# Four attention layers on one core: the wide layers' output projection in half chunks, and scores issued in turn with transposes

## The reference

```
wide   (layers 0, 2): q = x Wq (16 heads of 64); k, v = ctx Wk, ctx Wv; logits get a masked bias on 4 columns
                      x = softmax(q k^T / 8 + bias) v  Wo + bo + x
narrow (layers 1, 3): q = rmsnorm(x) wq (16 heads of 32); 4 heads of k, v shared by 4 heads of q each
                      x = softmax(q k^T / sqrt(32)) v  wo + x
```

## Time and profile before

| | |
|---|---|
| median of three runs | 2080.31 us (2079.71 to 2081.9) |
| the profiled execution, its span | 2080.3 us |
| TensorE busy | 2042.1 us, 98% |
| VectorE, ScalarE, GpSimd busy | 1389.7, 966.4, 644.7 us |
| main stage: wide step without, with projection | 11.35 to 11.41 us, 33.85 us |
| narrow step with one projection chunk | 10.51 us |

### The profile page before, as it was taken

How to read it: one execution, slowest core, us unless ns; L and a number is a source line. 1 busy time by engine, 2 the same in 40 slices (tenths; PEclk the granted TensorE clock), 3 DMA queues, 4 the chain that set the end, 5 groups by cost and what they waited for, 6 DMA issues and landing times.

```text
span 2080.3 us, 31294 instructions
## 1 busy us (share of the span) xinstructions
PE 2042.1 (98%) x11546; PEld 1764.4 (85%) x11546; DVE 1389.7 (67%) x2408; ACT 966.4 (46%) x1814; POOL 644.7 (31%) x519
## 2 busy tenths in 40 slices
PE   8999999999999998999999999999999989999998
PEld 8999988888888887788888888888888877888887
DVE  5322365775577557788888676557755775888886
ACT  3222354544355344555555454335443553555553
POOL 1000043311232244454443341223112533444441
PEclk9999999999999999999999999999999999999999
DMA  7889742222122222343333332212221232333332
GB/s 190 174 178 206 189 96 67 67 65 78 51 72 69 71 70 78 86 105 98 90 94 94 104 97 64 75 56 67 65 78 51 72 90 66 80 87 89 86 72 83
DMA packets 262537, 191.02 MB, mean 92 GB/s; under 512 B 197522, under 2 KB 199986, under 8 KB 259826
## 3 DMA queue, kind: packets, MB, share of 16 engines
q1 hardware_dynamic: 262386, 189.03, 35.6%
HBM read 132.66 MB, written 56.26 MB: 91 GB/s over the span
## 4 chain that ended last, share of the span: by engine, by line
PE 89%; DVE 6%; DMA 1%; ACT 1%; issue 1%; SPq 1%; POOL 0%; DVEq 0%; ACTq 0%; POOLq 0%
PE acc_bank L878 11%; PE acc_bank L261 8%; PE acc_bank L263 8%; PE acc_bank L262 8%; PE q_bank L836 8%; PE q_bank L840 8%; PE q_bank L838 8%; PE t_bank L858 7%; PE ctx_bank L261 3%; PE ctx_bank L262 3%; PE ctx_bank L263 3%; PE s_bank L799 2%; PE s_bank L261 2%; PE s_bank L796 2%; PE s_bank L802 2%; PE s_bank L263 2%
## 5 line engine op out<-in xcount | busy, mean ns | idle before, releaser
L1313 POOL TENSOR_TENSOR prob<-prob,rinv 128x1232 f32<-128x1232 f32 x128 | 288.5, 2254 | 1026.2 <-DVE rinv L1197 1026.2
L1055 ACT ACTIVATE q_s<-q_bank 128x512 fp32r<-128x512 f32 x192 | 115.0, 599 | 499.1 <-PE q_bank L840 494.8
L878 PE MATMUL acc_bank<-pT_s,vals_s 128*128 128x512 f32 x1024 | 337.8, 415 | 0.0
L1155 DVE TENSOR_REDUCE mx<-s_bank 128x4 f32<-128x308 f32 x512 | 240.2, 469 | 122.1 <-PE s_bank L263 63.2
L836 PE MATMUL q_bank<-x_s,w_s 128*128 128x512 f32 x768 | 318.9, 415 | 0.0
L840 PE MATMUL q_bank<-x_s,w_s 128*128 128x512 f32 x768 | 313.4, 408 | 0.0
L838 PE MATMUL q_bank<-x_s,w_s 128*128 128x512 f32 x768 | 312.8, 407 | 0.0
L261 PE MATMUL acc_bank<-o_s,w_s 128*128 128x512 f32 x752 | 303.6, 404 | 1.6 <-DVE o_s L1188 1.6
L263 PE MATMUL acc_bank<-o_s,w_s 128*128 128x512 f32 x752 | 296.7, 395 | 0.0
L262 PE MATMUL acc_bank<-o_s,w_s 128*128 128x512 f32 x752 | 296.7, 395 | 0.0
L1159 DVE TENSOR_TENSOR prob<-s_bank,mx 128x308 f32<-128x308 f32 x512 | 245.1, 479 | 27.4 <-DVE mx L1155 1.4
(11 more groups left out here) (107 smaller groups left out, 4095.5 us busy)
## 6 DMA issues: line engine op xcount, KB each, us to landing
stream<-x_back SPq DMA_DIRECT2D x128, 256.0 KB, 2.6
x_front<-stream SPq DMA_DIRECT2D x96, 256.0 KB, 3.3
x_back<-stream SPq DMA_DIRECT2D x96, 256.0 KB, 3.7
kvw_raw<-kvw SPq DMA_DIRECT2D x17, 1024.0 KB, 8.3
k_scr<-k_out SPq DMA_DIRECT2D x36, 308.0 KB, 10.4
keys_s<-k_scr SPq DMA_DIRECT2D x128, 77.0 KB, 2.5
v_scr<-v_out SPq DMA_DIRECT2D x8, 1024.0 KB
vals_s<-v_scr SPq DMA_DIRECT2D x512, 6.5 KB
```

The lines of the kernel that those rows point to most:

```text
L878: mm = pe.matmul(out, w, pT_s[:, part], start=i == mine[0] and part == 2 * n and w is v[0], stop=i == mine[-1] and w is terms[-1][0] and p ...
L1155: dve.tensor_reduce(top, scored, AX_X, ALU.max).then_inc(s_max, 1)
L1313: pool.tensor_tensor(view, view, rinv[:, slot].unsqueeze(2).broadcast_to([P, TILES * GH, CTX]), ALU.mult).then_inc(p_norm, 1)
```

## The change

The projection of a wide batch is cut into two halves of its sum (`h` = 0: `o_s` chunks 0 to 3, `h` = 1: chunks 4 to 7), each 4 x 3 matmuls. Half 0 of chunks 0, 1 runs 4 steps after the batch's first, then half 0 of chunks 2, 3, then half 1 of chunks 0, 1, then of 2, 3: two halves in every wide step. VectorE adds each half to `x_back` by itself (the bias `bo` with the first). For the last wide batch the halves lie in the narrow steps 32 to 35 (96 to 99); `ahead` is gone. The order in a wide step is new on TensorE, ScalarE and VectorE: score tile 0 beside 12 queries, then 4 value matmuls, tile 1 and transposes 0 alternately, a half projection, 4 value matmuls, tile 2 and transposes 1 alternately, 12 queries, tile 3 and transposes 2 alternately, a half projection. Steps 0 and 1, which have fewer parts to run, differ a little.

```
 for h in range(kind(GROUPS * gb).halves):          # halves: 2 wide, 1 narrow
     for m in range(XC):
         if layer % 2 == 0: at = GROUPS * gb + 4 + 2 * h + m // 2
         else:              at = GROUPS * gb + 5 + (m if b < B - 1 else m // 2)
...
 # Plan.acc, wide step
+acc += values[:1] + projections[:1] + values[1:] + projections[1:]
...
 # TensorE
+def woven(small, turns):
+    for _ in range(6):
+        next(small, None)
+        next(turns, None)
...
+if a:
+    two = s + 1 < NU and kind(s + 1).name == "A"
+    beside(scores(s, 0), q, 12 if two else 0)
+    run(v, 4 if s >= 2 and kind(s - 2).name == "A" else 9)
+    woven(scores(s, 1), turns(0) if s > 1 else iter(()))
+    for item in projections[:1]: project(*item)
+    if s == 1: run(q, 12)
+    run(v, 4)
+    woven(scores(s, 2), turns(1) if s > 1 else turns(0))
+    run(q, 12)
+    woven(scores(s, 3), turns(2) if s > 1 else turns(1))
+    if s == 1: turned(2)
+    for item in projections[1:]: project(*item)
...
 # ScalarE, wide step
+bias(s, 2); next(q); split_o(s - 2, 0); turned(0); bias(s, 3); exps(s, 0); weights(); split_o(s - 2, 1); turned(1)
+bias(s + 1, 0); next(q); turned(2); exps(s, 1); bias(s + 1, 1); fresh_x()
...
 # VectorE, wide step
+late add_result; rest_t(s - 2, TWICE); tile_scores(s, 0); next(q); rest_o(s - 2, 0); tile_scores(s, 1); turned(0)
+add_result(first); rest_o(s - 2, 1); tile_scores(s, 2); turned(1); next(q); tile_scores(s, 3); denominators(s)
+add_result(second)
...
 # SyncE stores a chunk, and loads the next batch's, after its last half alone (plan.whole)
```

More of the change, by code:

```diff
@@ L134, in __init__ @@
                 queries.append(("stats", self.stats_at(s)))
[L135 to L141, removed]
+            projections = [("proj", *item) for item in self.projections(s)]
+            values = [("pv", s - 2, m) for m in range(kind(s - 2).Q)] if 0 <= s - 2 < NU else []
+            if s < NU and kind(s).name == "A":
+                acc += values[:1] + projections[:1] + values[1:] + projections[1:]
+            else:
+                acc += values + projections
         self.q = {item: n for n, item in enumerate(queries)}
@@ L149, in late, with whole @@
         found = self.projections(s) if s >= 0 else []
[L150 to L158, removed]
+        return found[-1:] if s < NU and kind(s).name == "B" else []
+    def whole(self, items):
+        return [(gb, m) for gb, m, h in items if h == kind(GROUPS * gb).halves - 1]
     def projections(self, s):
@@ L164, in projections @@
             layer, b = divmod(gb, B)
[L165 to L174, removed]
+            for h in range(kind(GROUPS * gb).halves):
+                for m in range(XC):
+                    if layer % 2 == 0:
+                        at = GROUPS * gb + 4 + 2 * h + m // 2
+                    else:
+                        at = GROUPS * gb + 5 + (m if b < B - 1 else m // 2)
+                    if at == s:
+                        found.append((gb, m, h))
         return found
@@ L947, in _, with turns @@
                 a = s < NU and kind(s).name == "A"
+                projections = plan.projections(s)
+                def turns(n):
+                    return turn(s - 1, n) if 0 <= s - 1 < NU else iter(())
                 def turned(n):
[L950 to L969, removed]
+                    run(turns(n), TILES)
+                if a:
[3 more added lines that the diff above has]
+                    woven(scores(s, 1), turns(0) if s > 1 else iter(()))
+                    for item in projections[:1]:
+                        project(*item)
+                    if s == 1:
+                        run(q, 12)
+                    run(v, 4)
+                    woven(scores(s, 2), turns(1) if s > 1 else turns(0))
+                    run(q, 12)
+                    woven(scores(s, 3), turns(2) if s > 1 else turns(1))
+                    if s == 1:
+                        turned(2)
+                    for item in projections[1:]:
+                        project(*item)
                     if plan.stats_at(s) is not None:
@@ L1257, in _ @@
                             tile_scores(s, t)
[L1258 to L1263, removed]
+                    for item in plan.late(s - 1):
+                        add_result(*item)
                     turned(0)
-                    if s < NU and not plan.ahead(s):
+                    if s < NU:
                         denominators(s)
@@ L1274, in _ @@
                     turned(2)
-                    for gb, m in plan.projections(s):
-                        if (gb, m) not in plan.late(s) and not plan.ahead(s):
-                            add_result(gb, m)
+                    for item in projections:
+                        if item not in plan.late(s):
+                            add_result(*item)
             for m in range(XC):
```

122 lines of the change are left out of this document (62 added, 60 removed).

## The result

| | before | after |
|---|---|---|
| median of the runs | 2080.62 us (20 runs, 2079.71 to 2082.41) | 2084.2 us (20 runs, 2080.45 to 2086.21) |
| ratio, 95% interval | | 1.0015 [1.0008, 1.0022] |
| span of the profiled execution | 2080.3 us | 2082.2 us |
| VectorE's additions of a chunk | 128 | 192 (64 instructions more on the page) |

A forecast was written before the change was run, and what follows sets the result against it. TensorE, busy 98% of the span, was taken as the bound, in wide layers through what one instruction costs. Terms -30.2 + 10 + 6 - 18.4 = -32.6 from 2080.3 gave 2048 us, range 2034 to 2080.

The forecast's parts named there:

- part 4: Costed at nothing: 64 more VectorE additions, SyncE's later loads and stores, GpSimd's work starting later in each step.
- part 2: New order's waits: none in steady wide steps, +10 us in steps 4, 31, 65, 68, 95, +6 us in steps 0 to 3.
- The prediction's own sign of being wrong: Steady wide steps coming out at 17 us or above, where 16.5 to 16.6 were forecast.
- Part 1: Wide steps' scores alternating with transposes: a score falls from 0.112 to 0.070 us, 12 per step, -30.2 us in all.
- rival A: Woven tiles: transposes' loads cost as much as the others, so alternating saves nothing; 2078 us, chance 0.17.
- The layout of a regular step: Wide step from T: GpSimd's product done at 6.6 us, first transpose at 7.4, slack 0.8; third group's rest 0.6.
- the loop through GpSimd: Steps 2 and 3, without projection: the chain of scores, exponential, denominators, GpSimd and transposes sets the step, 13.0 us against 11.4.
- Rival B: Wide steps' first transpose of tile 1 waits for a late chain through GpSimd; 2084 us, or 2152; chance 0.13.
- Part 3: Narrow steps 32 to 35 and 96 to 99, 24 matmuls each: TensorE bound, waits and slow clock gone, -18.4 us.
- C: Narrow steps from 32: the halves don't help, VectorE's chain bounds them as before; 2066 us, chance 0.12.

The follow-up runs named there:

- E4: Kernel before, its order kept, with the projection in half chunks, two at the end of each wide step: 2071.68 us, ratio 0.9955.
- E8: Control: kernel before with the last two wqB weight pieces split one step later: 2083.02 us, ratio 1.0012.
- E1: Changed kernel with the last two wqB weight pieces split one step later, in steps 30 and 94: 2073.12 us, ratio 0.9966.
- E7: Kernel before with half chunks in the old order and the last two wqB pieces one step later: 2062.77 us, ratio 0.9914.
- E11: Changed kernel with the second half projection ahead of tile 3's scores and transposes instead of behind them: 2192.15 us (one run).
- E6: Changed kernel with the wqB pieces one step later and the old order in wide steps 2, 3 and 67: 2061.33 us, ratio 0.9905.
- E10: Changed kernel, wqB pieces one step later, new order only in steps 5-29 and 69-93, old order with halves in other wide steps: 2046.5 us, ratio 0.9836.

## Why the prediction was wrong

**The step that failed is part 4**, "GpSimd keeps its order and starts each step's work later, as VectorE does", costed at nothing. The part asked itself what it costs if a cover is gone, and answered for SyncE alone. GpSimd's later work is what ScalarE waits for in steps 29 and 93, and what hid that wait was the projection that the change takes apart. The row stood in the trace of before, as an 8 us idle time of an engine that is busy 46% of the span; I had looked only at TensorE's waits, and what a cover hides doesn't stand there. The four steps behind it (30, 31, 94, 95) cost 18.8 us where +2.0 were forecast. E4 has the wait with the halves alone, in E8 the pieces gain nothing where the cover is in place, and E1 takes 10.5 of the 18.8 away by moving them. The 8.2 that are left in E1 lie in steps 31 and 95, where part 2 had laid waits of 2.0 each in the new order, and where the moved pieces still make the third group's rest 2 us late; with the pieces out of the way and the old order (E7) steps 30 and 31 take 32.39, less than before at equal work (22.42 + 11.23 = 33.65). The prediction's own sign of being wrong, regular steps of 17 us or above, didn't show: they came out at 16.64, and half of the miss lies in steps 30, 31, 94 and 95.

**Part 1, alternating: right in kind, too large.** 0.042 per pair was forecast, 0.030 is measured. TensorE's matmuls in one woven tile, and the loads of the same stretch:

```profile
502.92 0.24 PE L788 MATMUL s_bank<-keys_s,q_s 128*128 128x154 f32 x1
502.99 0.28 PE L850 MATMUL t_bank<-ident,rest 128*128 128x128 f32 x1
...
503.57 0.28 PE L850 MATMUL t_bank<-ident,rest 128*128 128x128 f32 x1
...
503.88 0.43 PE L254 MATMUL acc_bank<-o_s,w_s 128*128 128x512 f32 x1
```
```profile
503.13 0.14 PEld L850 LDWEIGHTS t_bank<-ident,rest 128*128 128x128 f32 x1
503.18 0.20 PEld L794 LDWEIGHTS s_bank<-keys_s,q_s 128*128 128x128 f32 x1
503.32 0.14 PEld L850 LDWEIGHTS t_bank<-ident,rest 128*128 128x128 f32 x1
503.37 0.20 PEld L788 LDWEIGHTS s_bank<-keys_s,q_s 128*128 128x128 f32 x1
```

A pair takes (503.57 - 502.99) / 3 = 0.193 us; forecast 0.179, rival A 0.221. The next load starts 0.05 after a transpose's, as part 1 had it from the earlier trace rows; but a transpose's load starts 0.14 after the score's ahead of it, not 0.11. What these 0.03 are no run shows; the 0.13 of the earlier trace rows, which part 1 kept as a bound, was the nearer row (the load ahead of it there, at 502.75, is a value matmul's, not a short one's). By the rule of the Trainium skill that part 1 weighed ("TensorE: Matmul & The Clock Gate", section "LDWEIGHTS (loading the stationary operand)"), a load's time follows from its column count alone, so that a transpose's load would take as long as a score's, both with 128 columns, and the pair would stay near the 0.221 of rival A; the trace differs, 0.193.

**Part 2: the regular steps don't wait, as forecast, and the starts cost more.** The layout of a regular step holds. T, the last score of tile 3, GpSimd's product, the third group's rest, and the first transpose behind them:

```profile
503.76 0.28 PE L794 MATMUL s_bank<-keys_s,q_s 128*128 128x154 f32 x1
507.93 2.25 POOL L1313 TENSOR_TENSOR prob<-prob,rinv 128x1232 f32<-128x1232 f32 x1 [11.09 <-DVE rinv L1196]
508.43 1.39 DVE L1173 TENSOR_TENSOR pT_s<-t_bank,pT_s 32x512 fp32r<-32x512 f32 x2
511.14 0.28 PE L850 MATMUL t_bank<-ident,prob 128*128 128x128 f32 x1
```

GpSimd's product ended 6.4 us after T (forecast 6.6), the first transpose came at 7.4 (7.4), and E11 puts the slack of the third group's rest at 1.1 (0.6). That no wide step waits in the old order holds for the regular ones alone: steps 0 and 1 waited 1.9 us before, steps 31 and 95 0.5 each. But steps 2 and 3 take 15.2, not the 13.0 of the loop through GpSimd. The chain of waits there (start, us, what) runs through another loop:

```profile
299.62 0.44 ACT s_bank L1031
300.06 0.64 ACT prob L1038
300.70 1.04 ACT w_s L1084 x2
301.74 0.49 ACT o_s L1074
...
302.25 0.69 DVE o_s L1187
302.94 0.39 DVE mx L1154
...
303.36 0.49 DVE prob L1158
303.87 0.43 ACT s_bank L1031
304.31 0.53 ACT q_s L1055
```

ScalarE and VectorE take turns through the whole step, in order: an exponential, two weight splits that the layout did not count (1.04 us), a value product's split and rest, a tile's maximum and subtraction, the bias. The bias that next step's first score needs (its 1.4 us wait is in the third row of the waits above) and the second query chunk's split stand at the end of it, so the rest of that query starts at 304.85, 2.2 us behind T (302.64), where the layout of a regular step has it on T. Rival B named this kind of thing ("two ScalarE items of 0.6 besides") and placed it in every step; it is there where TensorE has no projection to be busy with. Behind waits in these first steps lie stretches of 3.4 us at a granted clock of 0.5 (from 289.1 at the end of step 1, from 326.7 in step 4 and from 1227.8 in step 68), some 1.7 us lost in each, half of its length; part 2 had none. E6 shows that steps 2, 3 and 67 don't have these waits in the old order, and E10 shows it with the old order in all the first steps.

**Part 3: steps 32 to 35 take 59.3 us, not 54.8** (64.07 before). The slow clock is gone there, as forecast, but TensorE's half projections wait for VectorE's rests of the value products, 1.3 and 1.6 us in steps 32 and 33 and the same again in 96 and 97: the group of 5.7 us in the waits after. VectorE's first subtraction in step 32 came 1.0 us late, not 0.6. A group of the same kind stood in the trace before and I passed it over:

```profile
PE acc_bank L261 <- DVE o_s L1188: 1.6, 2, 1.3
```

E10 keeps these waits: 58.0.

Of the rivals B came nearest in time (its first figure is 2084), and by luck: it laid the loss into 56 wide steps, and the regular ones don't wait. A (2078) was wrong in mechanism, since the pairs do save; C is refuted, since the halves do help the narrow steps (E4).

## What to carry to other kernels

When a long block of work on the bounding engine is to be cut up, list what runs beneath it on every other engine, and look there for idle times of several us: each may be a wait that the block hides, as one was here, and comes up when the block goes. An order that is right in the regular step needs a layout of its own for the first and last steps of a stage, where parts are missing; where the order is written out by hand, the old one can stay there. Here that, and two weight pieces one step later, made 0.15% of loss into 1.6% of gain.

## What the hardware showed that I had not expected

A score matmul of 154 columns with a transpose behind it, 0.193 us for both, is neither the sum of the columns (0.179) nor of the two alone (0.221). And the granted clock fell to 0.5 (the 1.2 GHz level) behind waits that are short beside a step: for 6.8 us around the wait of 6.65, and for 3.4 us in step 4, where TensorE had waited 1.39, 1.64 and 0.34 us. Step 3 had waits of 1.44, 1.65 and 0.34 us and stayed at 1.00, so these rows don't tell which waits bring the clock down. In the main stage the changed kernel ran 23.8 us at 0.5, the kernel before 6.8; the regular steps of the changed kernel, without a wait, are at 1.00 throughout.
